# First attention of a gated cross-attention and expert kernel: some transfers change the queue that issues them

## What is computed

```
x = x + tanh(g_xattn[0]) * cross_attention_0(layernorm(x), ctx)      # 16 heads of 16
x = x + tanh(g_ffn[0])   * experts_0(layernorm(x))                   # 8 experts, 32 tokens of each batch, width 704
x = x + tanh(g_xattn[1]) * cross_attention_1(layernorm(x), ctx, ctx)
x = x + tanh(g_ffn[1])   * (routed_top2_of_7(h) + shared(h)),  h = layernorm(layernorm(x)) with scale and bias, width 1024
```

## Time and profile before

| | us |
|---|---|
| median of 3 runs (lowest, highest) | 896.84 (895.48, 896.87) |
| the profiled execution | 897.25 |
| its span, first to last instruction | 895.5 |
| first attention, about | 0 to 155 |
| first expert layer, about | 155 to 255 |
| second attention, about | 260 to 395 |
| shared and routed experts | 395 to 895 |

### The profile page before, as it was taken

How to read it: one execution, slowest core, us unless ns; L and a number is a source line. 1 busy time by engine, 2 the same in 40 slices (tenths; PEclk the granted TensorE clock), 3 DMA queues, 4 the chain that set the end, 5 groups by cost and what they waited for, 6 DMA issues and landing times.

```text
span 895.5 us, 17746 instructions
## 1 busy us (share of the span) xinstructions
PE 866.0 (97%) x5860; PEld 793.1 (89%) x5860; DVE 528.7 (59%) x1128; ACT 430.3 (48%) x939; POOL 283.0 (32%) x327
## 2 busy tenths in 40 slices
PE   8999999999969999999999999999999999999997
PEld 6777877999957778788888999999999999999986
DVE  5676774655567876747336473645647363645648
ACT  3555654877746565543225361625435261625431
POOL 6243422877765444124552002020110202020130
PEclk9999999999989999999999999999999999999999
DMA  5233237667630000020213232413322231422252
GB/s 201 66 116 107 79 109 263 203 208 219 199 105 7 7 6 5 6 96 1 77 52 100 70 106 68 129 51 94 93 85 68 80 115 51 124 74 99 58 185 100
DMA packets 74839, 86.95 MB, mean 97 GB/s; under 512 B 31188, under 2 KB 46962, under 8 KB 74668
## 3 DMA queue, kind: packets, MB, share of 16 engines
q1 hardware_dynamic: 70956, 79.86, 28.9%
q0 software_dynamic: 3552, 6.55, 2.2%
q10 hardware_dynamic: 288, 0.01, 0.0%
HBM read 64.08 MB, written 23.63 MB: 98 GB/s over the span
## 4 chain that ended last, share of the span: by engine, by line
PE 85%; SPq 7%; DVE 4%; issue 2%; ACT 2%; DMA 1%; POOL 0%; DVEq 0%; POOLq 0%
PE score L272 13%; PE score L274 13%; PE score L273 13%; PE bank_p L272 7%; PE bank_p L274 7%; PE bank_p L273 7%; PE bank L580 5%; SPq L333 5%; PE score L560 3%; PE bank_p L571 3%; PE bank L600 2%; PE bank L592 2%; PE bank L521 2%; PE bank L869 1%; DVE residual L1723 1%
## 5 line engine op out<-in xcount | busy, mean ns | idle before, releaser
L1125 ACT ACTIVATE silu<-score 128x366 f32<-128x366 f32 (+1 forms) x144 | 72.6, 504 | 277.9 <-PE score L274 277.9
L1483 DVE TENSOR_TENSOR prod<-silu,score 128x366 f32<-128x366 f32 (+1 forms) x144 | 82.1, 570 | 115.9 <-ACT silu L1125 115.9
L272 PE MATMUL score<-xe_hi,w_hi 128*128 128x366 f32 x448 | 149.3, 333 | 0.0
L274 PE MATMUL score<-xe_hi,w_lo 128*128 128x366 f32 x448 | 148.3, 331 | 0.0
L273 PE MATMUL score<-xe_lo,w_hi 128*128 128x366 f32 x448 | 148.3, 331 | 0.0
L1965 POOL DMA_INDIRECT slots_out<-yh,home_of x42 | 40.8, 972 | 336.6 <-DVE yh L1610 336.6
L272 PE MATMUL bank_p<-w_hi,hid_hi 128*122 128x256 f32 (+1 forms) x448 | 127.3, 284 | 0.7 <-DVE hid_lo L1491 0.7
L273 PE MATMUL bank_p<-w_lo,hid_hi 128*122 128x256 f32 (+1 forms) x448 | 125.6, 280 | 0.0
L274 PE MATMUL bank_p<-w_hi,hid_lo 128*122 128x256 f32 (+1 forms) x448 | 125.6, 280 | 0.0
L1794 POOL TENSOR_TENSOR w_lo<-raw,w_hi 128x512 fp32r<-128x512 f32 x62 | 82.6, 1363 | 26.3 <-ACT w_hi L944 19.7
L580 PE MATMUL bank<-v_blk,prob_t 128*128 128x136 f32 x640 | 81.9, 284 | 5.2 <-DMA v_blk<-values 4.8
(11 more groups left out here) (207 smaller groups left out, 1776.2 us busy)
## 6 DMA issues: line engine op xcount, KB each, us to landing
raw<-w_second_d SPq DMA_DIRECT2D x108, 256.0 KB, 2.7
raw<-w_first_d SPq DMA_DIRECT2D x72, 256.0 KB, 3.4
slot_rows<-yh SPq DMA_DIRECT2D x8, 771.0 KB, 3.4
yh<-slot_rows SPq DMA_DIRECT2D x8, 674.6 KB
v_blk<-values SPq DMA_DIRECT2D x256, 5.0 KB, 2.0
slots_out<-yh SPq DMA_DIRECT2D x8, 512.0 KB, 5.0
wa<-attn_w_d SPq DMA_DIRECT2D x8, 256.0 KB, 4.0
yh<-slots_out SPq DMA_DIRECT2D x4, 512.0 KB, 8.5
```

What stands on the lines that cost most here:

```text
L272: nc.tensor.matmul(o, a_hi, b_hi, start=start, stop=False)
L274: return nc.tensor.matmul(o, a_lo, b_hi, start=False, stop=stop)
L1125: nc.scalar.activation(silu[0:rows_n, buf, 0:width], src, ACT.Silu).then_inc(silu_done, 1)
L1483: nc.vector.tensor_tensor(prod[0:rows_n, buf, 0:width], silu[0:rows_n, buf, 0:width], up, ALU.mult).then_inc(gu_free, 1)
```

## The change

The helpers `matrix` and `zero_slots` get the issuing queue as an argument. Within the first attention, SP keeps the values, and ScalarE issues the nine weight pieces and the two matrices, in a new function `first_loads(n)` at the end of steps 0, 1, 2, and parts 0 to 4 of the zeros, at the end of steps 2 to 6. In each of these steps the new instructions stand behind `exps(g, 3)` (and, in step 0, behind the copy of the third group of values) and ahead of `norm2_t` and `high`. SP issues the last three parts of the zeros after its loop, where it issued two. The wait for `k_psum` ahead of the second key matrix goes (ScalarE has waited for it earlier in its own program); a wait for `zeros` (the memset of `yh`, the source of the zeros) comes in its place.

```diff
         @block.sync
@@ values_step
                 place_values(g, 1)
-                if early:
-                    for m in range(3 * n, 3 * n + 3):
-                        sp.dma_start(raw[:, m, :], w_first[0, m]).then_inc(raw_in[m], 16)
-                    if n == 1:
-                        matrix(1, V).then_inc(wv_in, 16)
-                    if n == 2:
-                        sp.wait_ge(k_psum, 1)
-                        matrix(1, K).then_inc(wk_in, 16)
-                if layer == 0 and (n is None or n == 2):
-                    zero_slots(b - 2)
@@ attention_loads
                 if layer == 0:
-                    zero_slots(B - 2)
-                    zero_slots(B - 1)
+                    for part in range(B - 3, B):
+                        zero_slots(sp, part)
         @block.scalar
@@ attention_step, behind exps(g, 3)
+                if layer == 0 and n in (0, 1, 2):
+                    first_loads(n)
+                if layer == 0 and (n is None or n == 2):
+                    zero_slots(act, b - 2)
                 if final_step:
                     warm_up(ACT.Silu)
                 elif two:
                     norm2_t(g - 2, layer == 0 and n == 2)
                     high(layer, g - 2, b - 2)
+            def first_loads(n):
+                for m in range(3 * n, 3 * n + 3):
+                    act.dma_start(raw[:, m, :], w_first[0, m]).then_inc(raw_in[m], 16)
+                if n == 1:
+                    matrix(act, 1, V).then_inc(wv_in, 16)
+                if n == 2:
+                    act.wait_ge(zeros, 1)
+                    matrix(act, 1, K).then_inc(wk_in, 16)
```

## The result

| | before | changed |
|---|---|---|
| median, us (lowest, highest; executions) | 896.68 (894.79, 900.8; 14) | 893.8 (891.96, 897.59; 14) |
| the profiled execution | 897.25 | 891.96 |
| its span | 895.5 | 890.2 |
| ratio, 95% interval | | 0.997 (0.9958 to 0.9982) |

The changed kernel is faster by 0.3%, 2.7 us by the ratio, between 1.6 and 3.8. The forecast was 4.7 us, a time of 892.1. That time is inside the range of 8 in 10 (890.0 to 895.8); the range that the prediction gave to its forecast alone, 890.3 to 893.5, is missed by 0.3. The profiled executions differ by 5.3 us, more than either; that the one pair of traces and the many executions disagree is the first thing to explain.

The account below looks back on a forecast made before the run. TensorE waits for v_blk values because SP's issue queue is too long. Gains 0.50 + 0.26 + 1.98 + 1.72 + 1.0 = 5.46 us, less 0.76 stall, give 4.7: 896.84 to 892.1 us; 8 in 10: 890.0 to 895.8.

Parts of the forecast that it names:

- rival 4: First attention: the wait was never SP's issues, so moving them does nothing, 896.8 us; chance 0.05.
- 1.1 us of waits for values: Profile after: TensorE's waits for v_blk fall from 4.8 us to about 1.1, none in steps 1 to 3.
- The tail of 1.72 us: Product at 74.42 us: slow matmuls at a lowered clock after the 1.98 wait; both go, gaining 1.72 us.
- Rival 1: Step 2: the new stall of 0.76 to 1.48 us brings the clock down, price 1.72, 893.8 us; chance 0.10.
- They land at 39.95, the wait of 0.50 goes: Batch 1's first-half values, near 41 us: 1.6 us sooner without the pieces, before TensorE is ready at 41.05.
- Rival 3: Values land late with pieces and zeros on another queue, at step 1 and the last wait: 2.5 us, 894.6; chance 0.08.
- The last wait: Batch 7's values, step 7: zeros leave SP's chain, gaining 1.0 us of 1.78; some 0.8 us stays.
- ScalarE's cost: End of steps 0 to 6: new issues cost TensorE nothing, except a 0.76 us stall in step 2 (bounds 0 to 1.48).
- the middle of the three cases: Step 2: ScalarE issues while the exponential (0.72 us) runs, stalling TensorE 0.76 us; otherwise 1.48 or nothing.
- the prediction's own cover: Step 2, time ScalarE's issues can take without stalling TensorE: 1.55 us, plus the exponential's 0.72, together 2.27.
- Two queues that take turns: ScalarE's issues wait while SP issues; gain eaten from 1.09 us per issue, no change at 1.10, 897.0 us; chance 0.15.
- the loop's 0 to 0.4: Steps 3 to 6, ScalarE's zero issues: nothing, at most 0.4 us in each of four steps, 1.6 in all.

Follow-up runs that it names:

- pieces alone: Against the changed kernel, zeros back on SP; ScalarE issues only the nine weight pieces and two matrices: 894.19 us, ratio 0.9976 to the kernel before.
- zeros alone: Against the changed kernel, pieces and matrices back on SP; ScalarE issues only the zeros of steps 2 to 6: 895.87 us, ratio 0.9993.
- loads later: Against the changed kernel, ScalarE's loads of steps 0 and 1 moved behind the next step's first exponential; measured twice: 892.54 and 892.11 us, ratios 0.9956 and 0.9955.
- step 2's loads on SP: Against the changed kernel, the four loads of step 2 back on SP, behind its place_values(g, 1): 894.49 us, ratio 0.9986.
- both: Against the changed kernel, ScalarE's loads of steps 0 and 1 some 3 us later and step 2's four loads back on SP: 893.35 us, ratio 0.9971.
- best: Against the changed kernel, loads of steps 0 and 1 behind the next step's first exponential, step 2's behind its second exponential: 891.75 us, ratio 0.9952.
- zeros in seven issues: Against the changed kernel, zeros of steps 3 to 6 cut into seven ScalarE issues per step, same bytes: 903.51 us, ratio 1.0078 to the changed kernel.

## Why the prediction came out as it did

All traces in one table. Waits of TensorE are in us, s for `stage`; the last column is the time from the first product with the values to the first matmul of the expert layer, and in brackets the same less a clock tail of 1.7. The first product's own wait is in no column.

| kernel | near 41 | near 57 | near 73 | last batch | clock falls at | stretch |
|---|---|---|---|---|---|---|
| before | 0.50 | 0.26 | 1.98 | 1.78 | 74 | 127.4 (125.7) |
| before, again | 1.63 | 0.33 | 0.64 | 1.60 | 133 | 127.0 (125.3) |
| changed | 0.83 | 0.44 s | 0 | 0.29 | no | 122.6 |
| changed, again | 0 | 0.43 s | 0 | 0.78 | no | 121.9 |
| changed, third | 1.92 | 0.43 s | 0 | 0.68 | 43 | 125.5 (123.8) |
| pieces alone | 1.46 | 0 | 0 | 1.71 | no | 123.8 |
| zeros alone | 0.38 | 2.13 | 0 | 0.92 | 59 | 126.0 (124.3) |
| loads later (two traces) | 0, 0 | 0.43 s, 0.45 s | 0, 0 | 1.02, 0.60 | no | 122.2, 122.2 |
| step 2's loads on SP | 0 | 0 | 1.44 | 0.49 | no | 122.7 |
| both | 0 | 0 | 1.48 | 1.05 | no | 123.5 |
| best | 0 | 0 | 0 | 0.76 | no | 121.4 |
| zeros in seven issues | 1.14 | 0.43 s | 1.97 s, and 1.94, 1.28, 1.32 s later | 0 | 75 | 131.8 (130.1) |

1. **What bounds the kernel: right.** TensorE's waits for `v_blk` were the price, and SP's queue of issues their cause. With issues gone SP waits for TensorE, and the waits near 57 and 73 us for values are gone in all three traces of the changed kernel. The pieces and matrices alone bring most of it (0.9976). That rules rival 4 out, for which moving issues does nothing. The sign that was to show it, 1.1 us of waits for values, was met to the tenth by luck: forecast as 0.28 at the first product and 0.8 at the last batch, measured as 0.83 near 41 us and 0.29 at the last batch.
2. **The tail of 1.72 us: wrongly counted as certain.** This is the term that was mis-sized. It stood in the one trace, and the text took it into the sum in full. About half the executions of the kernel before have it. For the changed kernel 5 of 34 have a mean clock of 0.994. As an estimate: 0.47 - 0.15 = 0.32 of the executions, times 1.6 us, is 0.5 us and not 1.72. It is a rough one: 13 of the 34 have a lower mean clock still, for which the start of the second attention is reason enough (below), and a tail can hide in them. Of the three traces one has a tail. Rival 1 had the clock fall at the new stall in step 2, at 893.8, the very time that was measured; but no trace of the changed kernel has a fall there, the one fall is near 43 us. The row with 1.78 us of idle time at clock 1.00 stood in the prediction; it should have told that the clock's fall isn't a property of the wait.
3. **"They land at 39.95, the wait of 0.50 goes": the step that failed.** SP issues them about as early as predicted (the last at 37.84; 38.34 and 39.06 in the other traces, 39.45 and 40.44 in the kernel before), but the last one lands after 3.38, 4.27 and 2.67 us. Rival 3 named this mechanism and this place, with 0.08, as a case beside the forecast; it was a part of what happened. With the same loads 3 us later the wait is gone in both traces, and the kernel is 0.15% faster (0.9956 and 0.9955 against 0.9970, 0.9974, 0.9968; 892.11 against 893.82 us on one chip): shown, by the landings, the waits and the time.
4. **The last wait: right.** Forecast some 0.8, measured 0.29, 0.78, 0.68. The pieces alone leave it at 1.71, the zeros alone bring it to 0.92, so it was the zeros, as the prediction had it.
5. **ScalarE's cost: right in kind and near in size.** Steps 0, 1 and 3 to 6 cost TensorE nothing; step 2's stall was to be 0.76 and is 0.43 to 0.44. The issues start with the exponential, as the middle of the three cases had it, and last 2.80 us, not 3.03. By the prediction's own cover that leaves 2.80 - 2.27 = 0.53.
6. **Two queues that take turns: it did not come.** In step 2 of the first trace ScalarE's issues of 0.44 to 0.49 us run while SP's last 0.55 to 0.60. ScalarE's pieces take a little longer than on SP, where the median was 432 ns. ScalarE's, in ns (min/median/max):

```profile
L1059 ACTq DMA_DIRECT2D raw<-w_first_d x9: 334/450/458, 26.3 to 53.9; - x9
```

That is far from the 1.09 us at which the gain would be gone. It isn't so everywhere: in the last version (`best`) three of ScalarE's issues beside SP's, from 45.80 us, last 0.60 to 0.62 us, and near 42.7 one issue of SP's lasts 1.74 us and this one beside it 1.64:

```profile
42.74 1.64 ACTq L318 DMA_DIRECT2D wa<-attn_w_d  x1
```

The Trainium skill, page "Perfetto Trace Analysis", section "DMA Instruction — HWDGE (DVE, Sync)", has the generator locked for exclusive use during an issue. Whether such a lock makes these issues longer no run tells, for long ones occur without a neighbour too: SP's for the values, alone in the kernel before, last up to 1.46 us (at 44.74), and 1.73 in its second trace (at 28.75).

The sum itself: the range 890.3 to 893.5 comes out at 890.5 to 893.3 by its own terms, and the loop's 0 to 0.4 in it is 0 to 1.6 in the part on ScalarE.

Without tails, the stretches say 125.5 before and 122.8 after (means of two and three traces), 2.7 us; the forecast without its tail was 2.98. With the 0.5 us for the tails that is 3.2, within the measured 1.6 to 3.8. The two profiled executions showed 5.3 because the one before had a tail and the one after had the fastest time of its 14.

**What stays open.** The start of the second attention, which the change doesn't touch, takes 14.8 to 15.2 us in some traces and 16.2 to 16.6 in others, by how long the clock stays at the 1.2 GHz level there. The five traces with a mean clock of 0.992 or less have the long one, the eight others the short one. The kernel before, run again, had the low mean clocks that go with it in 8 of 12 executions, and beside it in 4 of 35. The changed kernel had them in 13 of 34, the kernel before beside this study's kernels in 7 of 68. Why, no run here tells, and it blurs every comparison: as an estimate, (0.38 - 0.10) x 1.4 us (16.4 against 15.0) = 0.4 us of the changed kernel's gain are hidden by it. Nor is it shown why the idle times of 1.60 and 1.92 us brought the clock down and those of 1.71, 1.78 and 1.94 did not.

## What to carry to other kernels

A queue of small transfers is bound by its issues (0.63 us each here, against 2.0 us for a landing), and the cure is to take other issues off it; but the transfers taken off still share the DMA engines, so put them where no small transfer is being awaited, not only on an engine that has time. Issues on a compute engine are free while it idles and cost about their full time from there on: for that engine, count issues, not bytes. And a term that stands in one trace as a fall of the clock belongs into the sum with a probability, not in full.

## What the runs showed of the hardware

- Small transfers on one queue are slowed by large ones on another. In step 2 of the changed kernel, with pieces, a matrix and zeros in flight, four of the values' transfers (SP's issues in ns min/median/max, first and last start; time to landing):

```profile
L342 SPq DMA_DIRECT2D v_blk<-values x4: 553/597/1684, 54.4 to 56.3; - x4
...
DMA to landing us min/median/max: 4.6/5.9/6.1
```

  against 1.9/2.0/4.5 over the whole first attention of the kernel before. The Trainium skill, page "DMA: Bandwidth & Descriptors", section "Queues, rings and completion order", says that each DMA engine serves the queues it has work for in turn, a packet at a time; the trace agrees in so far as transfers of one queue land late while the other's are in flight. It needs no second queue: the 4.5 of the kernel before belongs to the first small transfer behind SP's own zeros, at 65.73.
- Issues grow longer behind large transfers: the last of the four above takes 1.68 us and not 0.60, after ScalarE's issues are over (55.87). In the kernel before SP's issues behind its own zeros last 1.17 to 1.24 us.
- ScalarE's queue starts an issue with the activation ahead of it (both at 53.07) and not when that has ended, so the time of that activation, 0.72 us, is cover. What the exponential waits for, the issue waits for too. Where the exponential is held up only by its own engine's earlier work, the issue even starts ahead of it, as in `best`:

```profile
41.25 0.34 ACTq L1061 DMA_DIRECT2D raw<-w_first_d  x1
41.48 0.73 ACT L983 ACTIVATE prob<-prob 128x616 f32<-128x616 f32 x1
```
- The same kernel's clock falls at different places in different executions: the kernel before at 74 us in one trace and at 133 in the other, the changed kernel at 43 in one of three and in the other two not at all in the first attention.
